# A linear-attention and feed-forward layer on one core: the ring of masked scores goes from four buffers to three

## The chip, the core and the metric

The kernel runs on one core of one Trainium2 chip. The metric is the device time of one execution in microseconds (us), from which the median of three runs is given. The profile is of one further execution of the same program. Engines are named as the profile does: PE is the matrix engine (PEld its weight loads), DVE the vector engine, ACT the scalar engine, POOL GpSimd, SP the engine that issues most DMAs.

## What is computed

The input is 4 sequences of 1024 tokens, 512 wide. After a layer norm, two branches run: a feed-forward block with a router, whose result passes through a SiLU and becomes a gate `g`, and a gated delta-rule attention with 16 value heads on 8 key heads. The output is `x + s * g`. The attention, which is where the change lies, is this recurrence per head and token:

```
S = S * exp(g_t)
delta = (v_t - k_t S) * beta_t
S = S + k_t (outer) delta
o_t = (q_t * scale) S
```

before it come a projection, a causal convolution of four taps, a SiLU and the norms of `q` and `k`; behind it a gate `silu(z)`, an RMS norm and the output projection.

## The kernel before

The kernel has two parts, one after the other. `feed_forward` takes the first 1.1 ms and is not touched. `attention` takes the rest. It works in two passes over the weights (two groups of eight value heads), each over four sequences. The data is cut in *tiles* of 256 tokens (32 tiles in all), each tile in two chunks of 128 tokens, and each chunk in two *units* of four heads: 128 units in all, four to a tile. Here units are numbered 0 to 127 in the order of the program; unit n is the one of the (n+1)-th instruction at L1620. Unit 84 to 87 are the four of tile 21.

The recurrence is evaluated in chunk form. A unit n goes through these steps:

- `scores`: PE multiplies keys with keys and with queries (L1581) into one PSUM bank.
- `decay`: DVE runs a scan over the rates (L1590) into the single buffer `gam`, ACT takes the exponential (L1598).
- `lower`: DVE multiplies one half of the scores with `gam` into `ltm` (L1613). POOL sets its diagonal (`unit`, L1625) and ACT converts it to 16 bits (`high`, L1633).
- `attend`: DVE multiplies the other half of the scores with `gam` into `pt` (L1620). `pt` is the ring that the change touches. `attend` is also the last reader of the bank of the scores and of `gam`: the scan of unit n+1 waits for it.
- the inverse: a chain of short 16-bit matmuls (L1675) with small DVE and ACT operations between them, from `start` (L1696) over six levels, an error and three corrections, to `third` (L1791), which writes `yfin`. Two such chains run side by side, one for even units and one for odd ones. `start` of unit n waits for `third` of unit n-2.
- the core: `recall`, `query`, `eps`, `learn`, `answer` (L1800, L1823, L1847, L1861, L1887), where the state of the recurrence is carried from unit to unit. `answer` (L1887) is the only reader of `pt`.
- the output: norm, transposition through DRAM, and the output projection (`out`, L1989).

Besides, each tile has work of its own, the *tile lane*: 16 projections of four matmul steps (`product`, L1250) and a projection of `z` by seven products (L1333, the "z chain" and "z pairs"). The tile lane and the scores share three PSUM banks in a fixed cycle. Every projection, every `scores` and both halves of the `z` work are one *turn*, and a turn may start when the turn three places before it has been emptied. The list of turns per tile stands in `fills`:

```python
fills = [*(("product", i) for i in range(4)), ("scores", 1), *(("product", i) for i in range(4, 2 * GK)), ("product", V0), ("product", V0 + 1),
         ("product", V0 + 2), ("scores", 2), ("product", V0 + 3), ("product", V0 + 4), ("product", V0 + 5),
         ("product", V0 + 6), ("scores", 3), ("product", V0 + 7), ("zchain",), ("zpairs",), ("scores", 0)]
```

so that `scores` of units 1, 2 and 3 of a tile stand among the projections of the next tile, and `scores` of unit 0 behind the `z` work.

The order of the instructions of every engine is fixed before the kernel runs, by a list scheduler (`planned`). It has a duration for each step (`TAKES`), the waits of each step (`after`) and a few lags. At each point it gives the engine that is free first the ready step with the longest remaining path; on PE it keeps short 16-bit steps and long ones apart by a penalty. The steps of one lane keep their order, the lanes are mixed freely. The waits on the chip are separate semaphore waits, written in each step's function. For the ring both say the same thing: `attend` of unit n comes behind `answer` of unit n - PIPE.

```python
("dve", "attend"): [("act", "decay", n), ("pe", "scores", n), ("pe", "answer", n - PIPE)],
("dve", "decay"): [("dve", "attend", n - 1), ("act", "decay", n - 2)],
```

Of the kernel before, what the change touches and what calls it, by code (L numbers as in the profile page):

```python
# [62 lines left out]
SERIES = 9  # L63
G_LNB, G_PAST, G_END, G_ALL = range(4)
KINDS, SLOTS = 4, 3
PIPE = 4
BLK = 32
NBLK = P // BLK
SCALED = 64.0
# [989 lines left out]
def attention(nc, bank, r, x, w_qkvz, w_out, xt_d, g_d, gate_d, row_d, vd, xd, kd, bd, part_d, out):  # L1059

    with ExitStack() as ctx:
        def sb(name, shape, dtype=F32):
            return ctx.enter_context(nc.sbuf_tensor(name, shape, dtype))
# [24 lines left out]
        wz, xz = sb("wz", [P, 3, KH, HEADS * P]), sb("xz", [P, 4, KH, P])  # L1088
        ltm, pt = sb("ltm", [P, HEADS, P]), sb("pt", [P, PIPE, HEADS, P])

# [524 lines left out]
        def dve_attend(dve, n):  # L1615
            dve.wait_ge(s["gam_sb"], n + 1)
            dve.wait_ge(s["kq_ps"], n + 1)
            if n >= PIPE:
                dve.wait_ge(s["o_ps"], n - PIPE + 1)
            dve.tensor_tensor(by_key(pt[:, n % PIPE]), by_key(gam[:]), scored(n, 1), ALU.mult).then_inc(s["pt_sb"], 1)  # L1620

# [256 lines left out]
        def pe_answer(pe, n):  # L1878
# [7 lines left out]
            for h in range(HEADS):  # L1886
                i = pe.matmul(split(b_s1)[:, :, h], pt[:, n % PIPE, h], reps[:, :, h], start=True, stop=True)  # L1887
            i.then_inc(s["o_ps"], 1)
# [215 lines left out]
        def after(engine, kind, *i):  # L2104
# [88 lines left out]
            if kind == "out":  # L2193
# [10 lines left out]
                ("dve", "lower"): [("act", "decay", n), ("pe", "scores", n), ("pool", "low", n - 1)],  # L2204
                ("dve", "attend"): [("act", "decay", n), ("pe", "scores", n), ("pe", "answer", n - PIPE)],
                ("pool", "unit"): [("dve", "lower", n)],
# [306 lines left out]
```

## Time and profile before

| | |
|---|---|
| median of three runs | 4027.89 us (4027.06 to 4028.06) |
| the profiled execution's own time | 4027.15 us |
| its span, first to last instruction | 4025.4 us |
| PE busy | 3942.0 us, 98% |
| weight loads busy | 3015.1 us, 75% |
| DVE busy | 3097.8 us, 77% |
| ACT busy | 2298.9 us, 57% |
| POOL busy | 1500.1 us, 37% |
| granted clock of PE, mean | 0.994 |

The busy time of an engine is the sum of its instructions. That of PE is modelled for the ends of its matmuls, so 98% says that PE has something in hand nearly always, and not that its array is full. The span is 1.75 us shorter than the execution's own time.

### The profile page before, as it was taken

The numbers are of one execution on the slowest core, as the hardware profiler recorded it, in microseconds if no ns is written. First come the engines' busy times: TensorE is split into PE (matmuls) and PEld (weight loads), VectorE is DVE, ScalarE is ACT, GpSimd is POOL, SyncE is SP. The second block draws the span as 40 slices with busy tenths as digits, with TensorE's granted clock in tenths as the row PEclk, the third lists the DMA queues.
The fourth block names the chain that finished last, engine by engine and source line by source line (L and its number), as shares of the span: only waits on it lengthen the run. The fifth ranks groups of instructions, "written<-read, shape, count | busy, mean of one in ns | idle before, by whom it ended". The sixth has DMA issues, their size and how long they took to land. (4 is left out here: it accounts for less than half of the span.)

```text
span 4025.4 us, 83987 instructions
## 1 busy us (share of the span) xinstructions
PE 3942.0 (98%) x29304; PEld 3015.1 (75%) x29304; DVE 3097.8 (77%) x6628; ACT 2298.9 (57%) x5920; POOL 1500.1 (37%) x1881
## 2 busy tenths in 40 slices
PE   7999999999999999999999999999999999999998
PEld 6788787887677777777777776777777777777775
DVE  6666666666588888888888887887888888887885
ACT  2222222222377777667677766767776767677674
POOL 2332232322233333333333334334444444444444
PEclk9999999999999999999999999999999999999999
DMA  4212111120443435344344454444444445445443
GB/s 151 49 37 50 25 50 38 38 50 19 146 113 96 102 100 132 98 104 103 104 106 102 106 143 127 107 132 119 123 115 122 116 120 131 132 116 134 121 109 97
DMA packets 813542, 400.79 MB, mean 100 GB/s; under 512 B 475584, under 2 KB 738752, under 8 KB 813120
## 3 DMA queue, kind: packets, MB, share of 16 engines
q1 hardware_dynamic: 777024, 340.17, 32.4%
q10 hardware_dynamic: 36096, 55.24, 5.0%
q8 instruction: 234, 3.83, 0.4%
q14 instruction: 188, 1.54, 0.1%
HBM read 242.57 MB, written 152.63 MB: 98 GB/s over the span
## 5 line engine op out<-in xcount | busy, mean ns | idle before, releaser
L1250 PE MATMUL bank<-xtile,wt 128*128 128x259 f32 x4096 | 1077.1, 391 | 6.5 <-PEq L766 2.5
L1250 PEld LDWEIGHTS bank<-xtile,wt 128*128 128x128 f32 x4096 | 727.2, 191 | 136.1 <-issue 43.7
L1732 ACT ACTIVATE xyinv<-bank 128x512 f16<-128x512 f32 x768 | 449.9, 590 | 222.0 <-PE bank L1675 217.9
L1989 PE MATMUL bank<-wot,xnt 128*128 128x512 f32 x1024 | 530.9, 610 | 4.0 <-DMA xnt<-x_scratch 3.2
L1708 DVE TENSOR_TENSOR wlev<-bank,mask 128x256 f16<-128x256 f32 x768 | 315.9, 415 | 164.1 <-PE bank L1675 161.1
L1379 DVE SCALAR_TENSOR_TENSOR vraw<-bank,taps,vraw 128x256 f32<-128x256 f32 x768 | 361.1, 476 | 33.8 <-ACT vraw L1372 19.9
L550 PE MATMUL bank<-hb,wt 128*128 128x128 f32 x2816 | 375.5, 277 | 8.3 <-DVE part L590 5.7
L550 PEld LDWEIGHTS bank<-hb,wt 128*128 128x128 f32 x2816 | 349.4, 194 | 17.6 <-issue 7.2
L1675 PEld LDWEIGHTS bank<-xyinv,lth 128*128 128x128 f16 x3584 | 202.6, 98 | 166.4 <-issue 88.3
L613 POOL TENSOR_TENSOR hid<-part 128x256 f32<-128x256 f32 x176 | 139.4, 792 | 473.3 <-ACT part L605 473.3
L1639 POOL TENSOR_TENSOR ltl<-ltm,lth 128x512 f16<-128x512 f32 x128 | 155.7, 1216 | 416.4 <-ACT lth L1633 416.4
L627 PE MATMUL bank<-wd_sb,hid 128*128 128x512 f32 x704 | 304.8, 592 | 0.0
L550 PE MATMUL bank<-hb,comb 128*128 128x128 f32 x2112 | 296.0, 277 | 0.0
L1675 PE MATMUL bank<-xyinv,lth 128*128 128x64 f16 (+1 forms) x3584 | 259.5, 196 | 20.8 <-ACT xyinv L1732 19.5
L1650 POOL TENSOR_TENSOR kend<-ktok,gts 128x256 f32<-128x256 f32 x224 | 140.3, 648 | 364.2 <-issue 363.8
L1675 PEld LDWEIGHTS bank<-wlev,xyinv 128*128 128x128 f16 x3072 | 172.6, 98 | 133.4 <-issue 96.2
L550 PEld LDWEIGHTS bank<-hb,comb 128*128 128x128 f32 x2112 | 266.8, 194 | 0.0
L605 ACT ACTIVATE part<-part 128x256 f32<-128x256 f32 x176 | 73.4, 417 | 332.2 <-DVE part L600 332.2
L627 PEld LDWEIGHTS bank<-wd_sb,hid 128*128 128x128 f32 x704 | 132.5, 190 | 160.7 <-issue 157.1
L1989 PEld LDWEIGHTS bank<-wot,xnt 128*128 128x128 f32 x1024 | 181.4, 192 | 82.6 <-issue 67.1
L1907 POOL TENSOR_TENSOR tq<-tq,zs 128x512 f32<-128x512 f32 x128 | 163.2, 1275 | 158.8 <-DVE tq L1900 142.3
L1675 PE MATMUL bank<-wlev,xyinv 128*128 128x64 f16 x3072 | 214.2, 193 | 4.2 <-DVE wlev L1708 4.1
(233 smaller groups left out, 8845.5 us busy)
## 6 DMA issues: line engine op xcount, KB each, us to landing
v_scratch<-vraw SPq DMA_DIRECT2D x64, 512.0 KB, 3.2
vtok<-v_scratch SPq DMA_DIRECT2D x512, 64.0 KB, 2.2
x_scratch<-tq SPq DMA_DIRECT2D x508, 64.0 KB, 1.8
xnt<-x_scratch SPq DMA_DIRECT2D x508, 64.0 KB, 2.5
grows<-row_scratch ACTq DMA_DIRECT2D x126, 256.0 KB, 3.7
k_scratch<-kraw SPq DMA_DIRECT2D x32, 512.0 KB, 2.7
ktok<-k_scratch SPq DMA_DIRECT2D x256, 64.0 KB, 2.1
b_scratch<-kraw SPq DMA_DIRECT2D x256, 64.0 KB, 1.8
```

Source lines behind the costliest of these rows:

```text
L550: i = pe.matmul(dst, w[:, k, f * P:(f + 1) * P], b[:, k], start=first and k == 0, stop=k == KH - 1, skip_group_check=True)
L613: pool.tensor_tensor(hid[:, f, :].rearrange("p (t c) -> p t c", t=2), part[:, n % 3, 0:2], part[:, n % 3, 2:4], ALU.mult).then_inc(s["hid_ ...
L627: i = pe.matmul(bank[6 + j % 2][:], hid[:, f, j * P:(j + 1) * P], wd_sb[:, f, :], start=(f == 0), stop=(f == FT - 1))
L1250: j = pe.matmul(b_p[:, 0:WIN], wt[:, k, c:c + P], xtile[:, par, k, :], **st)
L1379: dve.scalar_tensor_tensor(out=acc, in0=shaped(feats[i][0], tile_bank("product", q, prod_of[i])[:, tap:tap + TILE]), scalar=taps[:, group( ...
L1639: pool.tensor_tensor(ltl[:, n % 2], ltm[:], lth[:, n % 2], ALU.subtract).then_inc(s["ltl_sb"], 1)
L1650: i = pool.tensor_tensor(kend[:, r * REP:(r + 1) * REP].rearrange("p r (a x) -> p r a x", a=NBLK), ktok[:, tile % 2, cc, :, m * KPB + r].u ...
L1675: i = pe.matmul(dst[:, h * cols:(h + 1) * cols], lhsT(h), rhs(h), start=start and h == 0, stop=stop, skip_group_check=True)
L1708: dve.tensor_tensor(wlev[:, lv - 1].rearrange("p h (b t s) -> p h b t s", t=2, s=z)[:, :, :, 0, :], b_inv[p][:, 0:HEADS * P // 2].rearrang ...
L1732: act.activation(dst, b_inv[p][:].rearrange("p (a h b s) -> p a h b s", a=2, h=HEADS, s=z), ACT.Copy).then_inc(s[f"xy_sb{p}"], 1)
L1907: pool.tensor_tensor(tq[:, n % 2], tq[:, n % 2], zs[:, tile % 2, cc, m], ALU.mult).then_inc(s["xf_sb"], 1)
L1989: i = pe.matmul(b_o[:], xnt[:, h], wot[:, h], start=(h == 0), stop=(h == GV - 1))
```

## The change

One constant goes from 4 to 3. It is the number of buffers of `pt` (`[P, PIPE, HEADS, P]`, 2 KB per partition each), the distance in `attend`'s semaphore wait on `o_ps` (which `answer` raises), the index `n % PIPE` where `attend` writes and `answer` reads, and the distance in the planner's arc. No instruction is added or removed, and every duration of the planner stays. Since the planner works with the new arc, the order of the instructions on each engine is made anew, the DMA queues of SP and ACT too.

```diff
 G_LNB, G_PAST, G_END, G_ALL = range(4)
 KINDS, SLOTS = 4, 3
-PIPE = 4
+PIPE = 3
 BLK = 32
 NBLK = P // BLK
```

## Rows read from the trace of the kernel before

**Rows 1.** The page's head: span, and busy time of each engine.
```profile
span 4025.4 us, 83987 instructions
...
PE 3942.0 (98%) x29304; PEld 3015.1 (75%) x29304; DVE 3097.8 (77%) x6628; ACT 2298.9 (57%) x5920; POOL 1500.1 (37%) x1881
```

**Rows 2.** Windows: stretch, its length, then each engine's busy time (instructions), granted clock.
```profile
1129.00:3900.00 2771.00, 2736.13 (x21542) 2055.89 (x21540) 2288.42 (x4683) 1948.25 (x5053) 1114.91 (x1385) 1.00 0.44 115
3900.00:4025.00 125.00, 109.47 (x867) 74.34 (x865) 72.68 (x157) 59.06 (x182) 59.00 (x71) 0.96 0.42 106
```

**Rows 3.** The tile `pt`, stretch 0 to 3064.5: its instructions, first and last start.
```profile
L1887 PE MATMUL bank<-reps,pt x672: 270/275/356, 1164.3 to 3060.3; 128*128 128x128 f32 x168
...
L1620 DVE TENSOR_TENSOR pt<-gam,bank x87: 646/677/681, 1109.1 to 3045.0; 128x512 f32<-128x512 f32 x87
```

**Rows 4.** Timeline of DVE: start, length; `attend` and `lower` of units 86 to 88.
```profile
3044.95 0.68 DVE L1620 TENSOR_TENSOR pt<-gam,bank 128x512 f32<-128x512 f32 x1
...
3057.12 0.65 DVE L1613 TENSOR_TENSOR ltm<-gam,bank 128x512 f32<-128x512 f32 x1
...
3064.82 0.68 DVE L1620 TENSOR_TENSOR pt<-gam,bank 128x512 f32<-128x512 f32 x1
...
3092.77 0.69 DVE L1613 TENSOR_TENSOR ltm<-gam,bank 128x512 f32<-128x512 f32 x1
```

**Rows 5.** Timeline of PE: `scores` (L1581), `answer` (L1887), one step of `z` (L1333).
```profile
3040.18 1.11 PE L1581 MATMUL bank<-kqt 128*128 128x256 f32 x4
3055.94 1.03 PE L1581 MATMUL bank<-kqt 128*128 128x256 f32 x4
3059.55 1.05 PE L1887 MATMUL bank<-reps,pt 128*128 128x128 f32 x8
...
3066.39 1.96 PE L1333 MATMUL bank<-wt,xtile 128*128 128x512 f32 x4
...
3081.41 1.14 PE L1887 MATMUL bank<-reps,pt 128*128 128x128 f32 x8
...
3091.65 1.03 PE L1581 MATMUL bank<-kqt 128*128 128x256 f32 x4
3097.80 1.05 PE L1887 MATMUL bank<-reps,pt 128*128 128x128 f32 x8
3106.66 1.11 PE L1581 MATMUL bank<-kqt 128*128 128x256 f32 x4
3110.75 1.06 PE L1887 MATMUL bank<-reps,pt 128*128 128x128 f32 x8
...
3132.02 1.03 PE L1581 MATMUL bank<-kqt 128*128 128x256 f32 x4
...
3151.21 1.05 PE L1887 MATMUL bank<-reps,pt 128*128 128x128 f32 x8
```

**Rows 6.** Groups by line, 2000 to 3500: `unit` and `high`; count, busy, mean ns.
```profile
L1625 POOL TENSOR_SCALAR_AFFINE_SELECT ltm<-ltm 128x512 f32<-128x512 f32 x66 | 42.6, 646 | 92.7 <-DVE ltm L1613 92.6
L1633 ACT ACTIVATE lth<-ltm 128x512 f16<-128x512 f32 x65 | 41.0, 631 | 0.0
```

**Rows 7.** Timeline of DVE: the chain of unit 88, `start` and `third`.
```profile
3109.11 0.41 DVE L1696 TENSOR_TENSOR xyinv<-lth,mask 128x512 f16<-128x512 f16 x1
...
3152.53 0.69 DVE L1791 SCALAR_TENSOR_TENSOR yfin<-bank,xyinv 128x512 f32<-128x512 f32 x1
```

**Rows 8.** The same for unit 126, in the drain.
```profile
3954.66 0.41 DVE L1696 TENSOR_TENSOR xyinv<-lth,mask 128x512 f16<-128x512 f16 x1
...
3984.77 0.68 DVE L1791 SCALAR_TENSOR_TENSOR yfin<-bank,xyinv 128x512 f32<-128x512 f32 x1
```

**Rows 9.** Windows of L1675 alone, one tile's period.
```profile
3017.00:3108.70 91.70, 19.15 (x384) 17.74 (x384) 1.00 0.47 122
```

**Rows 10.** Windows of L1333 alone, from `attend` of unit 87 to `answer` of unit 84.
```profile
3064.80:3082.50 17.70, 8.09 (x16) 2.73 (x16) 1.00 0.66 188
```

**Rows 11.** Waits of the weight loads, 1129 to 3900: total us, times, longest.
```profile
PEld bank L1675 <- issue: 194.9, 675, 0.6
```

## The prediction

> **What bounds the kernel now.** I read the page first. PE is busy for 3942.0 of 4025.4 us, the next engine, DVE, for 3098 [rows 1]. The windows then give the attention alone: in the 2771 us from 1129 to 3900, PE is busy for 2736.1, so it lacks work for 35 us, and in the last 125 us, where the pipeline drains, for another 15.5 [rows 2]. The clock is at full in the first stretch. So the order of PE's instructions has next to no visible holes, and whatever the change does must show as new holes on PE, as fewer of the old 50 us of holes, or as another packing of the same instructions.
>
> Then I asked the tile `pt` how full its ring is. Before 3064.5 us `attend` has run 87 times, and `answer` for 672 matmuls, 8 to a unit, so 84 units [rows 3]. Units 84, 85 and 86 are in the ring, and at 3064.82 `attend` of unit 87 fills the fourth buffer [rows 4]. Its buffer had been given back by `answer` of unit 83 at 3060.60 [rows 5]. With three buffers it would have to wait for `answer` of unit 84, which ends at 81.41 + 1.14 = 3082.55 [rows 5]: 17.7 us later. I went through all 128 units in this way. In 118 of the 125 that can be compared, `attend` starts before the third-last `answer` is done, by a median of 5.7, 1.4, 15.7 and 18.7 us for the first to the fourth unit of a tile. The fourth buffer is in use nearly always. The change cannot be a change in name only.
>
> **The change, part by part.** The instructions are the same, so the sum has only waits and packing in it.
>
> *The write that must move.* `attend` of unit 87 slips from 3064.82 to 3082.55. What stands behind it is the scan of unit 88 (one `gam`), and the PE turn three places on in the fixed cycle of the three banks, which is the `z` pairs. If `lower` of unit 87 and the scores stay early, their bank is held, and PE's tile lane stops at the first step of the pairs. In the stretch that then has to be filled, 3064.8 to 3082.5, `z` takes 8.09 us of PE now [rows 10]. That is the upper end for this place: 8.1 us per tile, if no other lane fills it and it is not made up. The lower end is nothing, if the lane simply runs later against the core.
>
> *Does a later lane fit?* I lay the lane's own spacing on the new bounds. Its scores stand at 3040.18, 3055.94, 3091.65, 3106.66 and 3132.02 (units 86 to 90), the bounds are the ends of `answer` 84 to 87: 3082.55, 3098.85, 3111.81 and 3152.27 [rows 5]. One tile lasts 3132.02 - 3040.18 = 91.8 us.
> - From the end of `attend` 87 (3065.50) the `z` pairs and what stands between them take until 3091.65, 26.15 us. Starting from 3082.55 + 0.68 = 3083.23, scores of unit 88 come at 3109.4, 10.5 us behind their own bound of 3098.85: not held.
> - Scores of 89 follow by 15.0 us, at 3124.4; bound 3111.81: not held.
> - Scores of 90 follow by 25.4 us, at 3149.8; bound 3152.27: held for 2.5 us.
> - Scores of 91 follow by 15.8 us from the bound, at 3168.0. The bound is `answer` of 88, one tile after 84, at 3082.55 + 91.8 = 3174.4: held for 6.3 us.
> While a unit is held, the lane may still do the next two turns. Four projections and one scores last 15.0 us between scores of 88 and 89, so about 3.5 us a turn, some 7 us for two. Both holds are shorter. So the lane as a whole fits into the period when it runs about 18 us later against the core. This is the reason why I don't expect the 8.1 us.
>
> *What is late next.* The lane feeds the chain of the inverse. At 3109.4 scores of 88 would be done by 3110.5 and `lower` starts 1.1 us after the scores as now (3091.65 to 3092.77) [rows 4, 5], so it ends at 3111.2; `unit` and `high` take 0.65 and 0.63 [rows 6]: 3112.5. `start` of unit 88 now runs at 3109.11 [rows 7]. The chain of even units would start 3.4 us late. The other units of the tile have more room (`lower` of 87 is done at 3057.77, and its chain starts after 3090). The chain has no rest of its own between units: it takes 3152.53 + 0.69 - 3109.11 = 44.1 us for unit 88, and two units last 45.9. But it is elastic. In the drain, with PE nearly free, it takes 3984.77 + 0.68 - 3954.66 = 30.8 us [rows 8]. So the delay is paid only as far as PE finds nothing else in it.
> - Lower end: both chains use 19.15 us of PE in 91.7 [rows 9], one about a tenth. For 3.4 us that is 0.36 us of PE per tile, over 30 tiles 11 us.
> - Upper end: all of PE waits along, 3.4 x 30 = 102 us.
> I take 0.6 us per tile, near the lower end, since core, output projection, the other chain and the lane have work in hand: 18 us. The 30 tiles leave out the first and the last.
>
> *The two ends of the attention.* At the start `attend` of unit 3 is held by `answer` of unit 0 in the same way, once: nothing to 8.1 us, and I take 3. In the drain `attend` is followed by a PE turn no more; a late scan is the only cost and the chain's slack takes most of it: nothing to 3.4 us, I take 1. The feed-forward part keeps its order and its time. 2 KB per partition come free, and nothing uses them.
>
> Sum: 18 + 3 + 1 = 22 us on the profiled execution of 4027.15, which is 0.7 us under the median of the runs. Against the median: 4027.9 + 22 = 4050.
>
> The Trainium skill says in "Perfetto Trace Analysis", section "Identifying Performance Opportunities", that a gap that repeats on the engine that should be saturated can mean too little buffer for the next tile. By that rule the change goes the wrong way, which is the sign I have; the trace before has no such repeated gap (35 us in 2771), so with four buffers the rule finds nothing.
>
> **The rivals.**
>
> *Hidden (within 0.2%).* The lane runs 18 us later against the core and chains and core fill PE. For it: the lane's arithmetic above, and `lower` of 87 being done some 30 us before it is needed. Against it: 3.4 us at unit 88. Time 4020 to 4036, with the lower end of the chain's cost, 11 us, just outside.
>
> *The lane is blocked at the `z` pairs.* The greedy scheduler runs the lane ahead, since it picks by the longest remaining path and doesn't see the held bank, and then has only chains and core, which wait for their own results. Price: between half and all of 8.1 us per tile, 120 to 243 us, so 4150 to 4270. It decides if the other lanes have nothing ready. Against it: the output projection (L1989) and four other lanes.
>
> *Faster: another packing.* The order is new everywhere, and PE's time depends on it without any wait shown. Before the chain's weight loads stand 194.9 us of idle time with no releaser, in 675 places [rows 11], where a load of the 16-bit chain follows other work. If the new order takes chain steps together more often, a tenth fewer of them gives back 19.5 us, and a shorter lead may give some of the 15.5 us of the drain [rows 2]: 4027.9 - 19.5 - 5 = 4003 to 4019. It wins if the holes cost less than that. Nothing in the trace favours the one direction of packing over the other; a tenth more would cost as much, which widens my own case upward.
>
> The same page of the Trainium skill, section "Identifying the Most-Contended Engine", says that matmul busy time tells little of how near PE is to its limit and that the share of the weight loads is to be read. Here that is 2055.9 / 2771 = 74% [rows 2]. By that rule there is room in which an order could win time, and it speaks for this rival; PE's 98% speaks against it.
>
> **How the numbers follow.** A measurement of this kernel tells 0.2%, 8 us, from no change. Small new holes (my forecast, 4036 to 4150): 0.47. Blocked lane: 0.08. Hidden: 0.25. Faster packing: 0.20. So slower 0.55, within 0.2% 0.25, faster 0.20. The predicted time is that of the likeliest case, 4050. Its own range is from the lower end with nothing beside it, 4038, to 4027.9 + 102 = 4130. The range over all cases leaves out the blocked lane and the thin top of my own case (0.12 together) and the lower part of the faster one (0.08): 4010 to 4105.
>
> **What would show it.** In the changed trace `attend` of unit n never starts before `answer` of n-3 ends, and the lead of `attend` before `answer` falls from 86 us at unit 87 to at most about 3 x 22.9 = 69 on average. PE's idle time in the attention rises from 50 us by about 20. Waits of PE's L1333 and L1250 for `pt` appear if the lane is blocked. Waits of chain steps on PE for ACT and DVE grow if my step holds. The prediction is wrong if the idle time on PE stays and the total moves (packing), if the idle before L1675 loads changes by tens of us, or if PE gains holes of several us in each tile at L1333.

## The result, and the profile after

The kernel with three buffers takes 4060.95 us (median of four runs, 4057.94 to 4064.93), the one with four 4027.97 us. The ratio is 1.0078, with a 95% interval of 1.0065 to 1.0092: 33 us slower. The profiled execution took 4061.26 us at a span of 4059.5, 34 us more than before, and all of it lies in the attention. The granted clock of PE is 0.994 in both profiled executions, so the clock is not what sets them apart.

The two windows of the profile after (columns as in [rows 2]):
```profile
1129.00:3900.00 2771.00, 2717.19 (x21284) 2037.02 (x21283) 2281.80 (x4627) 1917.03 (x4998) 1126.49 (x1373) 1.00 0.44 114
3900.00:4059.50 159.50, 143.91 (x1135) 98.60 (x1133) 104.09 (x214) 81.84 (x228) 68.45 (x82) 0.96 0.41 104
```
In the same 2771 us PE gets through 21284 matmuls, where it did 21542 before [rows 2], and it has nothing in hand for 53.8 us, where it was 34.9. In the drain it idles for 15.6 us, as before (15.5). So 19 of the 34 us are idle time of PE in the full pipeline. PE's busy time over the whole span grows by another 15 us, from 3942.0 to 3957.1, with the same 29304 matmuls. No row says why the same matmuls keep PE busy for longer; the experiments come back to it.

The ring is where it was expected. The timeline of DVE after, `attend` of unit 87, `lower` and `attend` of unit 88 and `start` of 88, and that of PE, `answer` of units 84 and 85:
```profile
3089.05 0.68 DVE L1620 TENSOR_TENSOR pt<-gam,bank 128x512 f32<-128x512 f32 x1
...
3116.62 0.65 DVE L1613 TENSOR_TENSOR ltm<-gam,bank 128x512 f32<-128x512 f32 x1
3125.65 0.67 DVE L1620 TENSOR_TENSOR pt<-gam,bank 128x512 f32<-128x512 f32 x1
3132.26 0.77 DVE L1696 TENSOR_TENSOR xyinv<-lth,mask 128x512 f16<-128x512 f16 x1
```
```profile
3087.68 1.05 PE L1887 MATMUL bank<-reps,pt 128*128 128x128 f32 x8
...
3122.92 1.06 PE L1887 MATMUL bank<-reps,pt 128*128 128x128 f32 x8
```
`attend` of 87 starts 0.3 us after `answer` of 84, that of 88 1.7 us after `answer` of 85. Gone through over the units of the full pipeline, `attend` follows the third-last `answer` by medians of 0.8, 2.9, 0.4 and 0.3 us (first to fourth unit of a tile), and its lead before its own `answer` falls from 78 to 67 us. Every unit now stands at the edge of the ring. But the chain does not wait for `lower`: that of 88 ends at 3117.3 and its `start` comes 15 us later, as before. And DVE hardly ever meets the wait. What sat idle before `attend`, by the view of the tile `pt` from 1129 on:
```profile
  PE bank L1887: 3.8, 9
```
3.8 us in 9 places. So the wait by itself is next to free, and the question is which of the 19 us of holes belongs to what. The waits of PE, 1129 to the end (total us, times, longest), the first row in the profile before and the same row after:
```profile
PE bank L1675 <- ACT xyinv L1732: 17.8, 21, 3.8
```
```profile
PE bank L1675 <- ACT xyinv L1732: 31.0, 41, 4.5
```
All rows of PE's waits at the chain (L1675) together give 24.7 us before and 50.2 after. The row shown has about half of the rise (13.2 of 25.5 us); nearly all of the rest is at operands that DVE writes. In the row shown PE stands at a chain step whose operand ACT has not yet copied out of the bank (`merge`, L1732). What ACT itself waits for where it squares the tokens for the norms, in the profile before and in the one after:
```profile
ACT tsq L1430 <- DMA ktok<-k_scratch: 24.1, 23, 2.5
ACT tsq L1499 <- DMA qraw<-k_scratch: 18.6, 10, 5.3
```
```profile
ACT tsq L1499 <- DMA qraw<-k_scratch: 60.4, 22, 6.5
...
ACT tsq L1430 <- DMA ktok<-k_scratch: 30.7, 16, 3.7
```
This place was not in the sum. L1499 are the squares of the queries, L1430 those of the keys; both read data that has gone through DRAM. ACT's wait for the queries has tripled. The loads themselves are no slower: from the issue of the store of the queries to the landing of their last load it takes 9.6 us before and 9.8 after (medians over the 32 tiles). What moved are the squares. They start within 0.1 us of that landing, which is to say that ACT stood waiting, in 11 of 32 tiles before and in 24 after. ACT's loads of its function tables, 1.28 us each, went from 297 to 287, so they are not it either.

One such place in the changed kernel, the timelines of SP, of ACT and of PE:
```profile
2901.24 0.34 SPq L1481 DMA_DIRECT2D k_scratch<-qraw  x1
2903.88 3.64 SPq L1489 DMA_DIRECT2D qraw<-k_scratch  x8
```
```profile
2911.30 0.31 ACT L1499 ACTIVATE tsq<-qraw 128x128 f16<-128x128 f32 x1 [3.94 <-DMA qraw<-k_scratch]
...
2912.48 1.05 ACT L1732 ACTIVATE xyinv<-bank 128x512 f16<-128x512 f32 x2
```
```profile
2909.11 0.28 PE L1675 MATMUL bank<-xyinv,wlev 128*128 128x64 f16 x4
...
2911.02 1.02 PE L1989 MATMUL bank<-wot,xnt 128*128 128x512 f32 x2
2913.11 0.29 PE L1675 MATMUL bank<-xyinv,lth 128*128 128x64 f16 x4 [1.07 <-ACT xyinv L1732]
```
PE has finished the merges of both chains by 2909.4. ACT could copy them out at once, but the squares of the queries stand before them in its queue, and their load, whose eighth DMA has been issued by 2907.5, lands at 2911.3. ACT stands for 3.94 us, copies both at 2912.48, and PE, after three pairs of other matmuls, has nothing until 2913.11.

### The profile page after: what moved, and what is told of

Read it like the earlier page. It is cut to its first block and busy times, and to the rows that moved or that the text cites. A ratio compares the mean times of both kernels' runs of the same rounds, so it can differ in the third digit from the quotient of the medians.

```text
span 4059.5 us, 83977 instructions
## 1 busy us (share of the span) xinstructions
PE 3957.1 (97%) x29304; PEld 3019.9 (74%) x29304; DVE 3122.3 (77%) x6628; ACT 2289.8 (56%) x5910; POOL 1520.5 (37%) x1881
## 5 line engine op out<-in xcount | busy, mean ns | idle before, releaser
L1250 PE MATMUL bank<-xtile,wt 128*128 128x259 f32 x4096 | 1078.1, 392 | 7.7 <-PEq L766 2.5
L1250 PEld LDWEIGHTS bank<-xtile,wt 128*128 128x128 f32 x4096 | 732.5, 191 | 139.3 <-issue 52.7
L1732 ACT ACTIVATE xyinv<-bank 128x512 f16<-128x512 f32 x768 | 437.9, 590 | 237.2 <-PE bank L1675 235.0
L1675 PEld LDWEIGHTS bank<-xyinv,lth 128*128 128x128 f16 x3584 | 193.1, 98 | 170.6 <-issue 73.5
L1907 POOL TENSOR_TENSOR tq<-tq,zs 128x512 f32<-128x512 f32 x128 | 182.5, 1426 | 311.0 <-DVE tq L1900 271.5
L1675 PE MATMUL bank<-xyinv,lth 128*128 128x64 f16 (+1 forms) x3584 | 242.8, 197 | 36.9 <-ACT xyinv L1732 32.9
L1675 PEld LDWEIGHTS bank<-wlev,xyinv 128*128 128x128 f16 x3072 | 170.7, 98 | 117.4 <-issue 81.1
L1675 PE MATMUL bank<-wlev,xyinv 128*128 128x64 f16 x3072 | 208.7, 193 | 4.9 <-DVE wlev L1708 4.9
```

Of the source, the lines that this page charges most:

```text
L1250: j = pe.matmul(b_p[:, 0:WIN], wt[:, k, c:c + P], xtile[:, par, k, :], **st)
L1675: i = pe.matmul(dst[:, h * cols:(h + 1) * cols], lhsT(h), rhs(h), start=start and h == 0, stop=stop, skip_group_check=True)
L1732: act.activation(dst, b_inv[p][:].rearrange("p (a h b s) -> p a h b s", a=2, h=HEADS, s=z), ACT.Copy).then_inc(s[f"xy_sb{p}"], 1)
L1907: pool.tensor_tensor(tq[:, n % 2], tq[:, n % 2], zs[:, tile % 2, cc, m], ALU.mult).then_inc(s["xf_sb"], 1)
```

## The experiments

All kernels keep everything else. Ratios are to the kernel with four buffers run beside them, whose median was 4027.97 us for the changed kernel, 4030.45 for e1 to e4, 4033.41 for e5 to e8 and 4029.52 for e9 to e12, so the ratios can be compared and the medians only roughly. The two columns on waits are from 1129 us to the end: ACT for the loads of the queries and of the keys at its squares, and the sum of PE's rows at L1675.

| kernel | median us | ratio (95% interval) | ACT for queries, keys | PE at the chain |
|---|---|---|---|---|
| before (ring 4) | 4027.97 | 1 | 18.6, 24.1 | 24.7 |
| changed (ring 3) | 4060.95 | 1.0078 (1.0065 to 1.0092) | 60.4, 30.7 | 50.2 |
| e1 order of 3, ring 4 | 4060.26 | 1.0069 (1.0054 to 1.0084) | 57.9, 30.4 | 49.3 |
| e2 ring 2 | 4033.32 | 1.0005 (0.9996 to 1.0015) | 31.5, 3.9 | 30.6 |
| e3 ring 4, `lead` 0.48 | 4023.18 | 0.9980 (0.9970 to 0.9989) | 12.5, 24.7 | 18.9 |
| e4 ring 3, `lead` 0.48 | 4055.85 | 1.0058 (1.0043 to 1.0073) | 52.9, 38.0 | 43.5 |
| e5 ring 3, no wait for queries | 4030.62 | 0.9990 (0.9981 to 0.9999) | 0, 27.1 | 26.1 |
| e6 ring 4, no wait for queries | 4011.84 | 0.9945 (0.9930 to 0.9960) | 0, 24.0 | 18.1 |
| e7 ring 3, load of queries 6.7 | 4048.50 | 1.0039 (1.0025 to 1.0052) | 3.6, 48.1 | 41.1 |
| e8 ring 4, load of queries 6.7 | 4027.37 | 0.9984 (0.9974 to 0.9993) | 9.5, 35.9 | 28.9 |
| e9 ring 3, no wait for either | 4010.52 | 0.9950 (0.9937 to 0.9964) | 4.7, 0 | 16.5 |
| e10 ring 4, no wait for either | 4000.66 | 0.9925 (0.9911 to 0.9938) | 0, 0 | 10.4 |
| e11 ring 4, `lead` 0.48, queries 6.7 | 4005.85 | 0.9940 (0.9927 to 0.9952) | 3.3, 27.5 | 18.0 |
| e12 ring 4, load of queries 0.7 | 4051.25 | 1.0055 (1.0040 to 1.0070) | 35.0, 28.5 | 45.0 |

**The wait or the order (e1).** The planner's arc says 3, the buffers, the index and the semaphore wait say 4. The instructions of every engine stand in the order of the changed kernel.
```diff
-("dve", "attend"): [("act", "decay", n), ("pe", "scores", n), ("pe", "answer", n - PIPE)],
+("dve", "attend"): [("act", "decay", n), ("pe", "scores", n), ("pe", "answer", n - 3)],
```


> The planner is told the distance 3, so the order on every engine is that of the changed kernel, but the ring has four buffers and attend waits for answer of n-4. Theory A (the order made for three buffers costs, the wait itself is nearly never met: DVE stood before attend for answer only 3.8 us in the changed trace): as the changed kernel, 4055 to 4065 us. Theory B (the wait on the chip costs, since answers come later than planned): the loss goes, 4026 to 4040 us.

It is as slow as the changed kernel. Theory B is out: the memory and the wait on the chip cost nothing that can be measured, the order costs all of it. The opposite kernel, the old order with three buffers, was not run. By the old order `attend` of unit 87 stands on DVE (3064.82) ahead of other DVE steps that come before `answer` of 84 (3081.41); if that answer needs one of them, the kernel would hang. This is argued from the order, not shown.

**Less slack still (e2).**
```diff
-PIPE = 4
+PIPE = 2
```


> Ring, wait and planner at 2. Theory A (each buffer less takes slack from the closed loop answer, attend, lower, chain, core, answer): a lead of at most two periods, 46 us, against a chain that needs 44 us when PE is shared: the loss grows much faster than linear, over 60 us above the changed kernel, 4120 to 4250 us. Theory C (what was lost at 3 is an accident of one order of the list scheduler): 2 lies within 30 us of 3 on either side.

My theory (A) fell here; theory C, within 30 us of three buffers, holds at its edge with 27.6 us. With two buffers the lead is down to 44 us, DVE stands before `attend` for `answer` more often than with three, as the view of `pt` in this kernel shows,
```profile
  PE bank L1887: 12.6, 25
```
and the time is that of four buffers. In the full pipeline PE gets through 21508 matmuls in the window from 1129 to 3900, nearly the 21542 of before:
```profile
1129.00:3900.00 2771.00, 2739.34 (x21508) 2060.07 (x21508) 2284.47 (x4687) 1971.67 (x5076) 1138.76 (x1393) 1.00 0.45 115
```
So what is lost with three is not the slack of the ring. It is something in the order that comes out for three. The table has the sign of what: ACT stands before the two loads for 35.4 us here, less than the 42.7 of the kernel before and far less than the 91.1 of the changed one.

**Is it chance (e3, e4).** One planned duration that has nothing to do with the ring goes from 0.47 to 0.48 us, in both kernels.
```diff
-            ("act", "lead"): 0.47, ("act", "silu"): 1.06,
+            ("act", "lead"): 0.48, ("act", "silu"): 1.06,
```


> Ring of 4 as before; only the planner's duration of the ACT step lead goes from 0.47 to 0.48, so that another order with the same slack comes out. Theory A: within 8 us of before, 4020 to 4036. Theory C (any new order moves the time by tens of us): outside of that, as far as 4060.

> Ring of 3 with the same small edit of the planner's duration of lead. Theory A: the loss of the changed kernel stays, 4050 to 4072 us. Theory C: it can fall to that of before, 4030, or grow to 4090.

Both orders change, and both kernels win a little: 0.20% at ring 4, 0.20% at ring 3. The distance between three and four buffers stays at 0.78%. So orders do scatter by some 8 us, and the loss at three survives one other order. How different that order is can be read from the traces: e4 has the same instruction as the changed kernel in about half of the places in the order of DVE and of ACT (48% and 55%). One more order at each size does not rule out that a third would lose nothing.

**The waits of ACT (e5, e6).** The squares of the queries read the keys, which are in place long before, and wait for those. The order of each engine stays; what the kernel leaves out is the true norm of the queries, so its output is another. DVE gets a wait for the load that ACT no longer waits for, which is long past.
```diff
-            act.wait_ge(s["k_in"], K_IN * (q + 1))
...
-                i = act.activation(blocked(tsq[:, h]), qtok[:, cc, :, h], ACT.Square, accum_out=rnq[:, q % 2, cc, h:h + 1])
+                i = act.activation(blocked(tsq[:, h]), ktok[:, q % 2, cc, :, h], ACT.Square, accum_out=rnq[:, q % 2, cc, h:h + 1])
```


> The changed kernel, every engine's order kept, but ACT's squares of the queries read the keys that are long in place, so ACT doesn't wait for the load of the queries (the norms of the queries are those of the keys: the output is another). Theory D (ACT stands before these squares for a DMA, 60.4 us in 22 places, the chain's evictions behind it come late, and PE runs empty): most of the 33 us comes back, 4028 to 4045 us, and PE's idle time falls from 73 towards 54 us. Theory E (the 60 us of waits are only a sign of another order, and what costs is how the chain's matmuls are packed among the long ones): 4052 to 4062 us.

> The same with a ring of 4 and the order of before, where ACT waits 18.6 us for these loads. Theory D: a small gain, up to 10 us, 4018 to 4030 us. Theory E: as before, 4024 to 4036 us.

Ring 3 gains 0.88% and is as fast as the kernel before. PE's waits for `merge` fall to what they were, as the row of this kernel shows:
```profile
PE bank L1675 <- ACT xyinv L1732: 12.9, 20, 1.5
```
PE's idle time over the whole span falls from 102.4 to 76.6 us, and its busy time from 3957.1 to 3946.7 with every engine's order kept, so 10 of the 15 us of busy time that the change had added come of this wait as well. Theory E, that the packing alone costs, is out as the main cause.

Ring 4 gains too, 0.55%, more than I gave it. Its 18.6 us of ACT waits are worth 22 us of time (16 to 28 by the interval), so here such a wait costs about as much as it lasts. The fair reading is the difference: with both free of this wait, three buffers cost 0.45% in place of 0.78%. The wait for the queries carries 0.33%, 13 us, of the loss.

**Both waits gone (e9, e10).** The squares of the keys read the keys of before their way through DRAM as well, and those of the queries wait for the load of the keys, which is nearly always past (4.7 us in 2 places in e9). The cut shows the part on the keys.
```diff
-            act.wait_ge(s["k_in"], K_IN * q + KEYS_IN)
+            act.wait_ge(s["kqx_sb"], 2 * q + 1)
...
-                i = act.activation(blocked(tsq[:, h]), ktok[:, q % 2, cc, :, h], ACT.Square, accum_out=rnk[:, q % 2, cc, h:h + 1])
+                i = act.activation(blocked(tsq[:, h]), kraw[:, q % 2].rearrange("p (c a) h x -> p c a h x", c=CPT)[:, cc, :, h], ACT.Square, accum_out=rnk[:, q % 2, cc, h:h + 1])
```


> The changed kernel and its order; ACT's squares of queries and of keys both read data long in place, so ACT waits for neither load (the norms are of other numbers). Compared with the same edit at ring 4. Theory D (the loss is ACT standing before loads): the two differ by no more than the planner's own 4 us, so this one near 4010 to 4022 us. Theory F (next to it the shorter ring costs by its own, since attend now stands at the ring's edge in every unit and the core's slack is used up): 12 to 20 us stay between the two, this one near 4022 to 4032 us.

> The same edit at ring 4 with the order of before, where the waits for the keys are 24 us in 22 places. Theories D and F both: a little below the kernel with only the query wait gone (0.9945 of before), 4000 to 4012 us.

Now 0.25%, 9.9 us, lies between three and four. Theory D expected at most 4, theory F 12 to 20; the truth is between them, nearer to F's lower end. Of the 0.78%, the loads before the squares carry 0.53%, 21 us.

Where the rest sits, the heads of the two pages tell, e9 first:
```profile
PE 3943.8 (98%) x29304; PEld 3020.2 (75%) x29304; DVE 3124.2 (78%) x6628; ACT 2293.3 (57%) x5910; POOL 1519.5 (38%) x1881
```
```profile
PE 3934.9 (98%) x29304; PEld 3016.6 (75%) x29304; DVE 3099.4 (78%) x6628; ACT 2299.9 (58%) x5920; POOL 1498.9 (37%) x1881
```
The spans are 4009.1 and 3998.9 us, so PE's idle time is 65.3 and 64.0: 1.3 us of the 10.2 are idle time and 8.9 are PE's busy time. Without the waits for the loads, the order for three makes next to no more holes than that for four. That speaks against theory F, by which a core without slack would leave PE waiting, and for the packing of the same matmuls; what in the packing costs it is open.

**The planner's belief (e7, e8, e12).** The same waits, changed through the order alone. The planner takes 3.7 us for the load of the queries; these kernels say 6.7 and 0.7.
```diff
...
-            ("sp", "qload"): 3.7,
+            ("sp", "qload"): 6.7,
...
```


> Ring of 3; the planner believes that the load of the queries takes 6.7 us and not 3.7, so it puts the squares later. Theory D: ACT's wait for the load of the queries falls under 15 us and the time to 4028 to 4045 us. Theory E: another order, anywhere within 4045 to 4070 us.

> Ring of 4 with the same edit of the planner's duration. Theory D: 4018 to 4030 us, since little of this wait is left to win. Theory E: within 10 us of before on either side, 4018 to 4040 us.

> Ring of 4; the planner believes that the load of the queries takes 0.7 us in place of 3.7, so it puts the squares too early. Theory D: ACT's wait for these loads grows from 18.6 to 60 us or more and the time with it, 4040 to 4070 us. If the waits grow and the time stays within 8 us of before, theory D falls.

Ring 3 wins 0.39%, less than theory D expected: 4048.50 us lies outside its range and inside that of theory E. The wait for the queries goes, as D said, but that for the keys grows, from 30.7 us, as the rows of this kernel show:
```profile
ACT tsq L1430 <- DMA ktok<-k_scratch: 48.1, 24, 3.9
ACT tsq L1499 <- DMA qraw<-k_scratch: 3.6, 4, 2.2
```
In the other direction, ring 4 with a load believed to be short (e12) has the four buffers of before and loses 0.55%. The wait for the queries grew to 35 us and not to 60, and that for the keys from 24.1 to 28.5, so the time follows them in direction and not in proportion. Two other things moved in e12 too. PE's wait at the chain for another copy by ACT (L1768) went from 0.7 to 12.6 us. And the granted clock is 0.992 in place of 0.994, and its four runs lie in the order of their clocks: 4047.1 and 4050.3 us at 0.992, 4052.2 at 0.991, 4056.1 at 0.990. As an estimate, 0.2% of its span is 8 us, so about a third of the 22 us may be the clock's.

What follows the time better over all fourteen kernels is the last column of the table: the five at 1.0039 and above have 41 to 50 us at the chain, the nine at 1.0005 and below have 31 or less. The column measures PE itself, so it says where the time goes and not why.

**A faster one (e11).** The two edits of e3 and e8 together.

> The two edits of the planner's durations that gave 0.9980 and 0.9984 of before each, together: lead 0.48 and load of the queries 6.7 us, ring of 4. Theory D: the waits for the queries under 10 us, 4012 to 4024 us, the fastest kernel that computes the reference. Theory C (orders scatter by some 10 us): 4015 to 4040 us.

4005.85 us, 0.60% under the kernel before, and it computes what the kernel before does. It goes below both ranges that I gave it. ACT waits 3.3 us for the queries, in 2 places, and PE gets through 21659 matmuls in the window from 1129 to 3900, where it was 21542.

## Why the prediction was right in its number and wrong in a step

The predicted time was 4050 us and the measured one 4061. The direction and the nearly always binding ring were foreseen. That the size came out near is luck: the term that carries it, 18 of 22 us, was put down to a delay that did not happen.

- *The ring binds nearly always.* Right: 118 of 125 units had to move, and after the change `attend` stands at the third-last `answer` in every position. The lead fell to 67 us, where at most 69 was foreseen.
- *The lane as a whole fits into the period when it runs later, and isn't blocked at the `z` pairs.* Right. In the changed trace no wait of L1333 for `pt` is left, and L1250 waits for it 1.6 us in 4 places. The rival at 4150 to 4270 is out.
- *What is late next: the chain of even units starts 3.4 us late.* This is the step that failed. `lower` of 88 ended 15 us before `start`, and `start` follows `third` of unit n-2 by medians of 1.7, 1.3, 2.7 and 0.1 us, where it was 1.7, 0.1, 0.2 and 1.1. The planner had moved the core as well, which my overlay of the old lane on the old answers could not see: `eps` follows `third` by medians of 0.8, 0.3, 0.9 and 0.5 us now, where it was 13.0, 1.1, 0.2 and 5.6. Ring 2 shows that a lead of 44 us costs nothing, so a late chain start can't be the price. What cost time is elsewhere: ACT standing before the loads for the norms, which carries 21 us of the 31 to 33. I had looked at PE's queue and at DVE's behind `attend`, and not at what the new order does to a queue that `attend` is not in.
- *Start and drain, 3 and 1 us.* The drain's idle time is 15.6 us against 15.5. In the first 81 us of the window, 1129 to 1210, PE is idle for 5.7 us against 5.6, so no `attend` held at the start shows there. The granted clock is 0.94 in that stretch against 1.00 before, and e1, with the same order, has 0.99 and is as slow over all.
- *About 20 us more idle time on PE.* Right in size, 19 us, by another cause. And only part of the loss; PE's modelled busy time grew by 15 us beside it, for which the sum had no term.
- *Faster by another packing.* The idle time before the chain's loads with no releaser was to tell: over the whole span it went from 205.2 to 186.1 us, so down, while the time went up. It is not the gauge that I took it for. Another order can win, though: e3 and e11 did, by having fewer chain steps whose operand is late.
- *The two rules of the Trainium skill.* Both stand in "Perfetto Trace Analysis". The one in "Identifying Performance Opportunities", that a gap which repeats can mean too few buffers, gave the right sign for the wrong reason: two buffers have no loss. The one in "Identifying the Most-Contended Engine", to read the share of the weight loads, left room for an order that wins, and the trace agrees so far: e11 is 24 us faster at 2064.84 / 2771 = 74.5%. But the share moves little, from 73.5% in the changed kernel over 74.2% before.

What stays open is 0.25%, 10 us, between e9 and e10, nearly all of it busy time of PE. The list scheduler's own finish, a number of the program and not of the chip, is 4.0 us later for three buffers than for four; but for two it is 18.3 us later, and the chip shows no such loss, so this does not explain it.

Why the change meets the loads can be followed one step further, again in the scheduler's own times. From the issue of the store to the squares it plans at least 9.0 us (0.45 and 3.7, a lag of 2.4 behind each, and 0.06). The chip takes 9.6 to 9.8 to the landing by medians, and up to 17.1, and 10.1 us in the place shown, from 2901.24 to 2911.30. So squares that are planned right behind the load come too early. In the order for three they are planned less than 1 us behind it in 22 of 32 tiles, in that for four in 7. Why the scheduler puts them there when the ring has three buffers stays open.

## What to carry to other kernels

With an order that is made ahead, a smaller buffer acts first through the order it produces, and its price can sit on an engine that never touches the buffer: split the two by giving the planner one distance and the chip the other. Look in each in-order queue for instructions that wait for a DMA, and ask what stands behind them; with the planned duration of one load 3 us shorter, and no buffer less, this kernel lost 0.55%, against 0.78% for the change. One more size of the same knob (here two buffers) is the cheapest test of a theory of slack.

## What the runs showed of the hardware that was not expected

An in-order engine that is busy for 56% of the span was where most of the loss arose. ACT's 18.6 us of waits before the squares of the queries were worth 22 us of the kernel's time in e6, and 60.4 us were worth 35 us in e5, with PE busy for 97 to 98% of the time. So such waits cost from half of themselves to about all.

A way through DRAM by one store and eight loads took 9.6 us by the median from the issue of the store to the last landing, and between 8.0 and 15.4 us over the 32 tiles of the kernel before.
